# Scan layer: who builds the diagonal blocks of B, GpSimd or ScalarE

## The chip, the core and the metric

The kernel runs on one core of a Trainium2 chip. The metric is the device time of one execution in microseconds (us). Three executions of the kernel before took 9809.74, 9821.51 and 9825.37 us; the median is 9821.51 us.

The engines go by the names of the profile: PE is TensorE (PEld its weight loads), DVE is VectorE, ACT is ScalarE, POOL is GpSimd, SP is SyncE, which here only starts DMAs. Each engine works through its own list of instructions in order and waits on semaphores that the others raise.

## What is computed

`x` is 4 images of 128 channels x 128 x 128 positions. Two layers are added to it, each on a group-normalised input (cut to what matters):

```python
# layer 0, along the 16384 positions of each image
xn = layernorm(gn(x)) * ln_w + ln_b
xin, z = split(xn @ W_in.T)
u = silu(causal_conv4(xin) + conv_b)                 # 256 channels
dt, Bm, Cm = split(u @ W_xproj.T, [8, 24])           # 8, 16 and 16 columns
delta = softplus(dt @ W_dt.T + b_dt)
h = exp(delta * A) * h + (delta * u) * Bm            # 256 channels x 16 states
y = (sum over states of h * Cm + u * D) * silu(z)
x = x + y @ W_out.T
# layer 1: a point-wise network of seven small products with leaky ReLUs; not touched by the change
x = x + sdf(gn(x))
```

## The kernel before

**Two stages per image.** Layer 0 walks the 16384 positions of an image in 32 chunks of 512 (T = 32), layer 1 walks the same 32 chunks after it. The change is in layer 0 alone. Chunks are numbered `t`, with a filling chunk ahead of each image.

**Units.** A chunk's 256 channels x 16 states are 16 units `m` (UNITS = 16). `unit(m)` gives `half`, `gp` (which half of the states) and `q`: units 0 to 3 and 8 to 11 have gp = 0, units 4 to 7 and 12 to 15 have gp = 1. Each unit goes through four engines:

- ACT `decay` (L699): two exponentials of 512 columns, the factor of h, into a ring of four buffers (DR). It may run up to four units ahead of the scan.
- PE `spread` (L446): 32 small products (64 instructions) that multiply delta*u by **diagonal blocks of B** and leave (delta*u)*B in one of two PSUM buffers. `spread(m)` may start when the scan of unit m - 2 is done, as that scan reads the same buffer.
- DVE `scan` (L927): two scans of 512 columns, the recurrence itself.
- POOL `times_c` (L815): one product of 1024 columns, h * C. PE adds these up over the states in `add_states` (L457), four units at a time.

**The order is written out by hand.** Each engine has a function `layer0` with a loop over m = 0 to 15 in which the work of the next two chunks is slipped in at fixed places. PE spreads and ACT decays two units ahead of the loop's m, so that m = 14 and 15 hold units 0 and 1 of the next chunk. What matters here:

- PE: m = 1 `add_states` and `z` half 1 (L401); m = 2 `c_dt_rows` (L406); m = 3 `center_it` (L372); m = 4 `variance` (L378); m = 5 `b_columns` (L414); m = 6 `step_size` (L423); m = 7, 9, 12 `add_states`; m = 8 `project_out` (L470); m = 9 `transpose_du` (L430); m = 11, 13, 15 `conv` (L389), of which m = 15 holds two calls; m = 12 `z` half 0 (L401).
- ACT: every second m `keep_last` (L703), the last state of a pair of units, which waits for their scans; m = 2 `carry_taps` (L633); m = 3 `silu_all` (L639 and L645, with a table load before and after); m = 4 `copy_rows` (L659 to L661); m = 5 `square` (L622); m = 6 `rstd` (L626, L628) and `copy_b` (L667); m = 7 `softplus` (L672 to L676); m = 10 `copy_du` (L681), which waits for `transpose_du`; m = 15 `diagonals` (L689).
- DVE: m = 3 and 12 `gate` (L935, L938); m = 7 `normed` (L911); m = 9 `step_size` (L919); m = 11 `residual` (L943, L945).
- POOL: m = 8 `step_u` (L823), delta*u, which waits for DVE's `step_size` and is what `transpose_du` needs; m = 11, 12 and 15 `diagonals` (L832).

Waits that the change and the prediction speak of: `z` half 1 writes the PSUM bank `qp` that ACT's first silu of z reads, and so waits for it:

```python
def z(t, i, h):
    ...
    if h == 1:
        pe.wait_ge(s_sz, 2 * t + 1)
```

`variance` waits for ACT's `square` (s_sq), ACT's second silu of z waits for `z` half 1 (s_z), `copy_du` waits for `transpose_du` (s_tr), and `transpose_du` waits for `step_u` (s_du).

**The diagonal blocks.** For each chunk b_t (128 x 2 x 4 x 8, written by `copy_b`) holds B's columns. `diag[gp]` is 128 x (4 columns c, 4 rows j, 128): for each c and j, two interleaved 64 x 64 diagonals. Six of the eight quarters (c = 0 to 3 of gp 0, c = 0 and 1 of gp 1) are written by three POOL products of 1024 columns, c = 2 and 3 of gp 1 by 16 ACT copies of 64 columns. A block may only be written anew when the chunk's last spread that reads it is done: for gp 0 that is unit 11 (s_set at 12), for gp 1 unit 15 (s_set at 16). The next chunk's spread of unit 0 waits for the blocks of gp 0, that of unit 4 for those of gp 1.

**SP's queue**, in one chunk: 16 DMAs that replicate delta (L284) in two groups, the load and the store of x (L257, L262), and twice four DMAs that replicate C (L275), of which the second four are needed by POOL's unit 4 of the next chunk.

Of the kernel before, what the change touches and what calls it, by code (L numbers as in the profile page):

```python
# [6 lines left out]
ALU = mybir.AluOpType  # L7
ACT = mybir.ActivationFunctionType

P = 128  # L10
# [4 lines left out]
UNITS = 16  # L15
# [19 lines left out]
def mamba_sdf_kernel(nc, x, w_in_t, conv_w_t, conv_b, ln_w, ln_b, w_cd_t, w_dt_t, a_log,  # L35
# [7 lines left out]
    with ExitStack() as ctx:  # L43
        def sb(name, shape, dt=F32):
            return ctx.enter_context(nc.sbuf_tensor(name, shape, dt))
# [26 lines left out]
        dmask = sb("dmask", [P, 64])  # L72
# [38 lines left out]
        b_t = sb("b_t", [P, 2, 4, 8])  # L111
# [7 lines left out]
        def halves(k):  # L119
# [3 lines left out]
        diag = [over(8 + 4 * i, 4).rearrange("p (c j k) -> p c j k", c=4, j=4) for i in range(2)]  # L123
# [22 lines left out]
        g = [over(40 + i, 1) for i in range(2)]  # L146
# [27 lines left out]
        s_xd, s_rows, s_bt, s_btc = sem("s_c_dt_rows"), sem("s_rows_copied"), sem("s_b_columns"), sem("s_b_copied")  # L174
        s_dt, s_ab, s_ed, s_sp, s_del, s_du = sem("s_dt"), sem("s_abs_dt"), sem("s_exp_dt"), sem("s_log_dt"), sem("s_delta"), sem("s_delta_u")
        s_tr, s_dut, s_dg, s_dga = sem("s_du_transposed"), sem("s_du_t_copied"), sem("s_diagonals"), sem("s_diagonals_by_scalar")
        s_cd, s_cr, s_dr = sem("s_c_stored"), [sem(f"s_c_replicated{i}") for i in range(2)], [sem(f"s_delta_replicated{i}") for i in range(8)]

        s_dA, s_set, s_scan, s_car, s_ch, s_sum = sem("s_decay"), sem("s_dBu"), sem("s_scan"), sem("s_state_carried"), sem("s_Ch"), sem("s_summed")
        s_sk, s_yg, s_o, s_res, s_st1 = sem("s_skip_added"), sem("s_gated"), sem("s_projected"), sem("s_residual"), sem("s_stats1")  # L180

        s_f1, s_f1l = sem("s_f1"), sem("s_f1_leaky")
        s_f2, s_f2l = sem("s_f2"), sem("s_f2_leaky")
# [7 lines left out]
        pe_counts = {s_cen: 1, s_var: 1, s_z: 2, s_cv: 2, s_xd: 1, s_bt: 1, s_dt: 1, s_tr: 1, s_set: UNITS, s_sum: 4, s_o: 1,  # L191
                     s_f1: 1, s_f2: 1, s_gp: 1, s_m2: 2 * NG, s_m3: NG, s_m4: NG // 2}
        act_counts = {s_sq: 1, s_lv: 1, s_rs: 1, s_c3: 1, s_sz: 2, s_u: 2, s_rows: 1, s_btc: 1,
                      s_ab: 1, s_ed: 1, s_sp: 1, s_dut: 1, s_dga: 1, s_dA: 2 * UNITS, s_car: UNITS // 2, s_f1l: 1, s_f2l: 1,
                      s_t2: 2 * NG, s_t3: NG, s_sg: 1}
        pool_counts = {s_du: 1, s_dg: 2, s_ch: UNITS}
        dve_counts = {s_xn: 1, s_del: 1, s_scan: 2 * UNITS, s_sk: 2, s_yg: 2, s_res: 1, s_st1: 1,
# [20 lines left out]
        def real(i):  # L218
            return 0 <= i < T
# [122 lines left out]
        def _(pe):  # L342
# [12 lines left out]
            for h in range(2):  # L355
                m = mm(ps[:, 3, 8 + h:9 + h], w_z[:, h * P:(h + 1) * P], lnb[:, :], start=True, stop=True)
# [76 lines left out]
            def spread(t, i, m):  # L433
                half, gp, q, e = unit(m)
                if m == 0:
                    pe.wait_ge(s_dut, t + 1)
                if m in (0, 4):
                    pe.wait_ge(s_dg, 2 * t + gp + 1)
                if m == 4:
                    pe.wait_ge(s_dga, t + 1)  # L440
                pe.wait_ge(s_scan, 2 * UNITS * t + 2 * (m - 1))
                for c in range(4):
                    for r in range(2):
                        for j in range(4):
                            dst = dbu[m % 2].rearrange("p (r s c g) -> p r c s g", r=2, c=4, g=2)[32 * j:32 * j + 32, r, c, :, :]
                            k = mm(dst,  # L446
                                   du_t[i % 2][64 * r:64 * r + 64, c, 32 * e:32 * e + 32], diag[gp][64 * r:64 * r + 64, c, j, :],
                                   start=True, stop=True)
                k.then_inc(s_set, 1)
# [154 lines left out]
        def _(act):  # L604
            A = nc.scalar.activation
# [57 lines left out]
            def copy_b(t):  # L663
                act.wait_ge(s_bt, t + 1)
                act.wait_ge(s_dg, 2 * t)
                act.wait_ge(s_dga, t)
                A(b_t[:, :, :, :].rearrange("p g c k -> p (g c k)"), pp[:, 1, 0:4 * NS], ACT.Copy).then_inc(s_btc, 1)  # L667

            def softplus(t):
# [8 lines left out]
            def copy_du(t, i):  # L678
                act.wait_ge(s_tr, t + 1)
                act.wait_ge(s_set, UNITS * (t - 1))  # L680
                A(du_t[i % 2].rearrange("p (k c) d -> p k (c d)", k=2), pp, ACT.Copy).then_inc(s_dut, 1)  # L681

            def diagonals(t):
                act.wait_ge(s_btc, t + 1)
                act.wait_ge(s_set, UNITS * t)
                for c in range(2, 4):
                    for j in range(4):
                        for gi in range(2):
                            d = A(diag[1][:, c, j, :].rearrange("p (s g) -> p g s", g=2)[:, gi, :], dmask[:, :], ACT.Copy,  # L689
                                  scale=b_t[:, 1, c, 2 * j + gi:2 * j + gi + 1])  # L690
                d.then_inc(s_dga, 1)

            def decay(t, m):
# [11 lines left out]
            def layer0(b, i):  # L705
                t = b * T + i + 1
                for m in range(UNITS):
                    if m + 2 < UNITS and real(i):
                        decay(t, m + 2)
                    elif m + 2 >= UNITS and real(i + 1):  # L710
                        decay(t + 1, m + 2 - UNITS)
                    if m == 0 and real(i - 1):
                        keep_last(t - 1, UNITS // 2 - 1)
                    if m > 0 and m % 2 == 0 and real(i):
                        keep_last(t, m // 2 - 1)
                    if m == 2 and real(i + 2) and i + 2 > 0:
                        carry_taps(t + 2, i + 2)
                    if m == 3 and real(i + 1):
                        silu_all(t + 1, i + 1)
                    if m == 4 and real(i + 1):  # L720
                        copy_rows(t + 1)
                    if m == 5 and real(i + 2):
                        square(t + 2)
                    if m == 6 and real(i + 2):
                        rstd(t + 2)
                    if m == 6 and real(i + 1):
                        copy_b(t + 1)
                    if m == 7 and real(i + 1):
                        softplus(t + 1)
                    if m == 10 and real(i + 1):  # L730
                        copy_du(t + 1, i + 1)
                    if m == 15 and real(i + 1):
                        diagonals(t + 1)

            def features(t):
                def first_layer():
# [68 lines left out]
        @block.gpsimd  # L805
        def _(pool):
            chunk_zero(pool, pool_counts)

            def times_c(t, m):
                half, gp, q, e = unit(m)  # L810
                if m % 8 in (0, 4):
                    pool.wait_ge(s_cr[gp], 64 * (t + 1))
                pool.wait_ge(s_scan, 2 * UNITS * t + 2 * m + 2)
                pool.wait_ge(s_sum, 4 * t + (m - CR) // 4 + 1)
                nc.gpsimd.tensor_tensor(hc[m % CR], H[:, m % HR, :, :], crep[:, 2 * gp:2 * gp + 2, :], ALU.mult).then_inc(s_ch, 1)  # L815

            def step_u(t, i):
                pool.wait_ge(s_del, t + 1)
                pool.wait_ge(s_u, 2 * t + 2)
                pool.wait_ge(s_tr, t)  # L820
                def fours(v):
                    return v.rearrange("p h (s c) -> p h s c", c=4)
                nc.gpsimd.tensor_tensor(du.rearrange("p h c s -> p h s c"), fours(delta), fours(u[t % 3]), ALU.mult).then_inc(s_du, 1)  # L823

            def diagonals(t, gp, part):
                if part == 0:
                    pool.wait_ge(s_btc, t + 1)
                    pool.wait_ge(s_set, UNITS * (t - 1) + 12 + 4 * gp)
                dst = diag[gp][:, 2 * part:2 * part + 2, :, :].rearrange("p c j (s g) -> p (c j) s g", g=2)
                one = dmask[:, :].rearrange("p (k s g) -> p k s g", k=1, g=1).to_broadcast([P, 8, 64, 2])  # L830
                col = b_t[:, gp, 2 * part:2 * part + 2, :].rearrange("p c (j s g) -> p (c j) s g", s=1, g=2).to_broadcast([P, 8, 64, 2])
                d = nc.gpsimd.tensor_tensor(dst, one, col, ALU.mult)  # L832
                if part == 1 or gp == 1:
                    d.then_inc(s_dg, 1)

            def layer0(b, i):
                t = b * T + i + 1
                for m in range(UNITS):
                    if real(i):
                        times_c(t, m)  # L840
                    if m == 8 and real(i + 1):
                        step_u(t + 1, i + 1)
                    if m == 11 and real(i + 1):
                        diagonals(t + 1, 0, 0)
                    if m == 12 and real(i + 1):
                        diagonals(t + 1, 0, 1)
                    if m == 15 and real(i + 1):
                        diagonals(t + 1, 1, 0)

            for b in range(B):  # L850
                for i in range(-1, T):
                    layer0(b, i)
# [273 lines left out]
```

## Time and profile before

| | us |
|---|---|
| median of three executions | 9821.51 |
| profiled execution, its own time | 9827.07 |
| its span | 9825.2 |
| TensorE clock granted, mean | 0.98 |
| busy: PE | 9314.5 (95%) |
| busy: DVE | 8993.4 (92%) |
| busy: ACT | 8370.6 (85%) |
| busy: POOL | 5791.9 (59%) |

The shares are means over two kinds of stage: POOL works in layer 0 only. The profiled execution lies 5.6 us above the median of the three, its span 1.9 us below its own time. A timeline row gives start, length, engine, line and operation, and in square brackets the idle time before it with what ended it; rows of like instructions are merged, and their number stands behind the x. Instructions of one engine overlap a little, so the pace of a group is read from one row's start to the next row's start.

### The profile page before, as it was taken

What the parts mean: (1) busy time and instruction counts of PE and PEld (TensorE: products, weight loads), DVE (VectorE), ACT (ScalarE), POOL (GpSimd) and SP (SyncE); (2) the same over time, 40 slices, a digit from 0 to 9 for tenths busy, and PEclk for the clock granted to TensorE, in tenths of its full rate; (3) what the DMA queues carried; (4) which work ended last, traced back from release to release, by engine and by line L of the source; (5) the groups of instructions that cost most, each with busy time, mean ns of one, the idle gap of its engine ahead of it and who ended that gap; (6) DMA issues with size and microseconds to landing.
All of it is one profiled execution on the core that took longest, in us unless ns stands there. A gap on an engine that the chain in (4) does not pass through costs nothing. (4 is left out here: it accounts for less than half of the span.)

```text
span 9825.2 us, 453859 instructions
## 1 busy us (share of the span) xinstructions
PE 9314.5 (95%) x201050; PEld 3949.9 (40%) x201050; DVE 8993.4 (92%) x10311; ACT 8370.6 (85%) x14741; POOL 5791.9 (59%) x2564
## 2 busy tenths in 40 slices
PE   7999998999899999899989999989998999998999
PEld 4555553222455555222245555522224555552222
DVE  6999998999699999899979999989997999998998
ACT  5888887999778888799978788879997887887999
POOL 5999993000699999300069999930007999992000
PEclk9999998999999999899999999999999999999999
DMA  3333331000233333100023333310002333321000
GB/s 102 81 82 88 83 84 44 31 31 27 66 81 87 84 81 86 40 31 31 27 69 87 81 81 84 84 43 29 30 27 73 87 81 82 87 80 32 21 22 18
DMA packets 377226, 605.60 MB, mean 62 GB/s; under 512 B 96962, under 2 KB 98148, under 8 KB 374756
## 3 DMA queue, kind: packets, MB, share of 16 engines
q1 hardware_dynamic: 370752, 574.99, 21.0%
q8 instruction: 1587, 26.00, 1.2%
q14 instruction: 371, 3.04, 0.1%
q10 hardware_dynamic: 4516, 1.57, 0.1%
HBM read 236.45 MB, written 71.30 MB: 31 GB/s over the span
## 5 line engine op out<-in xcount | busy, mean ns | idle before, releaser
L927 DVE TENSOR_TENSOR_SCAN arena<-arena,carried,ps 128x512 f32<-128x512 f32 x3968 | 4754.3, 1261 | 294.2 <-PE ps L446 287.9
L815 POOL TENSOR_TENSOR arena<-arena 128x1024 f32<-128x1024 f32 x2048 | 4798.2, 2382 | 148.1 <-PE ps L457 53.2
L975 DVE SCALAR_TENSOR_TENSOR arena<-arena,neg_p 128x512 f32<-128x512 f32 x4096 | 2762.8, 747 | 0.4
L699 ACT ACTIVATE arena<-arena,a_neg 128x512 f32<-128x512 f32 x4096 | 2662.8, 710 | 35.6 <-DVE arena L927 30.8
L446 PE MATMUL ps<-arena 64*32 64x128 f32 x131072 | 2335.8, 275 | 107.9 <-DVE arena L927 57.5
L754 ACT ACTIVATE arena<-ps,b2t 128x512 f32<-128x512 f32 x3840 | 2334.8, 699 | 70.3 <-PE ps L540 44.3
L446 PEld LDWEIGHTS ps<-arena 64*32 64x32 f32 x131072 | 1849.8, 106 | 1234.4 <-DVE arena L927 696.5
L823 POOL TENSOR_TENSOR arena<-arena 128x1024 f32<-128x1024 f32 x128 | 307.6, 2403 | 2969.7 <-DVE arena L919 2968.2
L540 PE MATMUL ps<-arena,w2s 32*32 32x512 f32 x32768 | 1578.5, 603 | 53.6 <-ACT arena L754 35.5
L761 ACT ACTIVATE arena<-ps,bm 128x1024 f32<-128x1024 f32 x1024 | 1165.3, 1138 | 6.1 <-PE ps L551 6.1
L551 PE MATMUL ps<-arena,m 64*32 64x512 f32 x16384 | 1120.7, 599 | 8.6 <-ACT arena L761 4.9
L457 PE MATMUL ps<-arena,sel 128*32 128x512 f32 x8192 | 1013.6, 612 | 37.6 <-POOL arena L815 21.1
L389 PE MATMUL ps<-xnf,w_conv 128*128 128x512 f32 x2048 | 1004.2, 623 | 16.6 <-DVE xnf L911 8.9
L540 PEld LDWEIGHTS ps<-arena,w2s 32*32 32x32 f32 x32768 | 366.6, 103 | 1191.0 <-issue 608.4
L832 POOL TENSOR_TENSOR arena<-dmask,b_t 128x1024 f32<-128x1024 f32 x384 | 735.0, 1915 | 0.0
L551 PEld LDWEIGHTS ps<-arena,m 64*32 64x32 f32 x16384 | 218.8, 104 | 909.3 <-issue 909.3
L681 ACT ACTIVATE arena<-ps 128x1024 f32<-128x1024 f32 x128 | 131.2, 1025 | 524.7 <-PE ps L430 524.7
L689 ACT ACTIVATE arena<-dmask,b_t 128x64 f32<-128x64 f32 x2048 | 504.0, 341 | 63.1 <-PE ps L446 63.1
L561 PE MATMUL ps<-arena,m 128*32 128x512 f32 x4096 | 546.3, 605 | 5.0 <-ACT arena L761 5.0
L389 PEld LDWEIGHTS ps<-xnf,w_conv 128*128 128x128 f32 x2048 | 364.0, 192 | 418.2 <-issue 402.8
L457 PEld LDWEIGHTS ps<-arena,sel 128*32 128x32 f32 x8192 | 228.2, 111 | 465.2 <-issue 432.7
L703 ACT ACTIVATE carried<-arena 128x4 f32<-128x4 f32 x1024 | 202.7, 198 | 248.1 <-DVE arena L927 241.2
(111 smaller groups left out, 6570.0 us busy)
## 6 DMA issues: line engine op xcount, KB each, us to landing
arena<-arena SPq DMA_DIRECT2D x4096, 64.0 KB, 2.0
arena<-c_d SPq DMA_DIRECT2D x1024, 128.0 KB, 2.9
xr<-in_x SPq DMA_DIRECT2D x128, 256.0 KB, 3.2
x_d<-xr SPq DMA_DIRECT2D x128, 256.0 KB, 3.3
xr<-x_d SPq DMA_DIRECT2D x128, 256.0 KB, 3.0
out<-arena SPq DMA_DIRECT2D x128, 256.0 KB, 2.0
xs<-in_x SPq DMA_DIRECT2D x96, 256.0 KB, 3.2
arena<-in_x SPq DMA_DIRECT2D x4, 2048.0 KB, 14.9
```

What stands on the lines that cost most here:

```text
L389: m = mm(pp[:, h, :], w_conv[:, k, h, :], xn[:, k:k + L], start=k == 0, stop=i > 0 and k == TAPS - 1)
L446: k = mm(dst, du_t[i % 2][64 * r:64 * r + 64, c, 32 * e:32 * e + 32], diag[gp][64 * r:64 * r + 64, c, j, :], start=True, stop=True)
L457: m = mm(y_ps[32 * q:32 * q + 32, :], sel[:, :], hc[(4 * k + q) % CR][:, gi, :], start=k % 2 == 0 and gi == 0, stop=k % 2 == 1 and gi == 1)
L540: m = mm(m2_ps[32 * q:32 * q + 32, j, :], w2s[32 * j:32 * j + 32, :], t1[k % 4][32 * j:32 * j + 32, q, :], start=True, stop=True)
L551: m = mm(m3_ps[32 * j:32 * j + 32, r, :], m3[64 * r:64 * r + 64, :], t2[k % 4][64 * r:64 * r + 64, j, :], start=True, stop=True)
L699: A(dA[(UNITS * t + m) % DR][:, gi, :], drep[:, e, :], ACT.Exp, scale=a_neg[:, e, 2 * gp + gi:2 * gp + gi + 1]).then_inc(s_dA, 1)
L754: a = A(t2[k % 4][:, j, :], m2_ps[:, j, :], ACT.Prelu, bias=b2t[:, GQ * k + j:GQ * k + j + 1], alpha=SLOPE)
L761: A(t3[k % 4], m3_ps, ACT.Prelu, bias=bm3[:, :], alpha=SLOPE).then_inc(s_t3, 1)
L815: nc.gpsimd.tensor_tensor(hc[m % CR], H[:, m % HR, :, :], crep[:, 2 * gp:2 * gp + 2, :], ALU.mult).then_inc(s_ch, 1)
L832: d = nc.gpsimd.tensor_tensor(dst, one, col, ALU.mult)
L927: V.tensor_tensor_scan(H[:, m % HR, gi, :], dA[(UNITS * t + m) % DR][:, gi, :], dbu[m % 2].rearrange("p (l g) -> p g l", g=2)[:, gi, :], 0 ...
L975: m = V.scalar_tensor_tensor(out=t1[k % 4][:, q, :], in0=g[par], scalar=neg_p[:, i:i + 1], in1=gs_[par], op0=ALU.max, op1=ALU.add)
```

## The change

Before, POOL made three products per chunk (at m = 11, 12, 15) and ACT sixteen copies (at m = 15). After, POOL makes two products (c = 0 and 1 of gp 0 at m = 11, c = 0 and 1 of gp 1 at m = 15), and ACT makes 32 copies in four calls of eight: gp 0 c = 2 at m = 12, gp 0 c = 3 at m = 13, gp 1 c = 2 at m = 14, gp 1 c = 3 at m = 15, each behind the decay (and keep_last) of its m. Each ACT call waits for b_t and for the old block's last spread. s_dga now counts four per chunk; PE's spread of unit 0 waits for 2 of them and that of unit 4 for all 4.

```diff
 # tensor, spread
                 if m in (0, 4):
                     pe.wait_ge(s_dg, 2 * t + gp + 1)
-                if m == 4:
-                    pe.wait_ge(s_dga, t + 1)
+                    pe.wait_ge(s_dga, 4 * t + 2 * gp + 2)
 # scalar
-            def diagonals(t):
+            def diagonals(t, gp, c):
                 act.wait_ge(s_btc, t + 1)
-                act.wait_ge(s_set, UNITS * t)
-                for c in range(2, 4):
-                    for j in range(4):
-                        for gi in range(2):
-                            d = A(diag[1][:, c, j, :].rearrange("p (s g) -> p g s", g=2)[:, gi, :], dmask[:, :], ACT.Copy,
-                                  scale=b_t[:, 1, c, 2 * j + gi:2 * j + gi + 1])
+                act.wait_ge(s_set, UNITS * (t - 1) + 12 + 4 * gp)
+                for j in range(4):
+                    for gi in range(2):
+                        d = A(diag[gp][:, c, j, :].rearrange("p (s g) -> p g s", g=2)[:, gi, :], dmask[:, :], ACT.Copy,
+                              scale=b_t[:, gp, c, 2 * j + gi:2 * j + gi + 1])
                 d.then_inc(s_dga, 1)
...
+                    if m == 12 and real(i + 1):
+                        diagonals(t + 1, 0, 2)
+                    if m == 13 and real(i + 1):
+                        diagonals(t + 1, 0, 3)
+                    if m == 14 and real(i + 1):
+                        diagonals(t + 1, 1, 2)
                     if m == 15 and real(i + 1):
-                        diagonals(t + 1)
+                        diagonals(t + 1, 1, 3)
 # gpsimd
-            def diagonals(t, gp, part):
-                if part == 0:
-                    pool.wait_ge(s_btc, t + 1)
-                    pool.wait_ge(s_set, UNITS * (t - 1) + 12 + 4 * gp)
-                dst = diag[gp][:, 2 * part:2 * part + 2, :, :].rearrange("p c j (s g) -> p (c j) s g", g=2)
+            def diagonals(t, gp):
+                pool.wait_ge(s_btc, t + 1)
+                pool.wait_ge(s_set, UNITS * (t - 1) + 12 + 4 * gp)
+                dst = diag[gp][:, 0:2, :, :].rearrange("p c j (s g) -> p (c j) s g", g=2)
...
                     if m == 11 and real(i + 1):
-                        diagonals(t + 1, 0, 0)
-                    if m == 12 and real(i + 1):
-                        diagonals(t + 1, 0, 1)
+                        diagonals(t + 1, 0)
                     if m == 15 and real(i + 1):
-                        diagonals(t + 1, 1, 0)
+                        diagonals(t + 1, 1)
```

## Rows read from the trace of the kernel before

**Rows 1.** Busy time in the scan stages of the four images (us; x instructions).

```profile
core 0: us, PE busy (x) PEld busy (x) DVE busy (x) ACT busy (x) POOL busy (x), PEclk, DMA share, GB/s
91.00:1513.50 1422.50, 1371.92 (x35300) 757.48 (x35306) 1339.73 (x1225) 1169.05 (x2281) 1385.32 (x613) 0.99 0.32 84
2528.10:3960.90 1432.80, 1375.56 (x35300) 757.69 (x35308) 1340.06 (x1225) 1169.32 (x2282) 1386.10 (x613) 0.99 0.31 83
4978.70:6409.10 1430.40, 1371.33 (x35300) 756.68 (x35308) 1339.05 (x1225) 1169.25 (x2281) 1385.01 (x612) 0.99 0.31 83
7426.40:8853.70 1427.30, 1371.66 (x35300) 756.75 (x35308) 1339.72 (x1225) 1169.22 (x2282) 1385.71 (x613) 0.99 0.31 83
```

**Rows 2.** Line L681 from 0 to 2000 us: durations (ns), first and last start.

```profile
L681 ACT ACTIVATE arena<-ps x32: 1024/1025/1027, 91.0 to 1513.5; 128x1024 f32<-128x1024 f32 x32
```

**Rows 3.** Timeline of POOL, one chunk.

```profile
1002.90 2.41 POOL L823 TENSOR_TENSOR arena<-arena 128x1024 f32<-128x1024 f32 x1 [0.18 <-DVE arena L919]
...
1016.43 1.93 POOL L832 TENSOR_TENSOR arena<-dmask,b_t 128x1024 f32<-128x1024 f32 x1
1018.29 7.04 POOL L815 TENSOR_TENSOR arena<-arena 128x1024 f32<-128x1024 f32 x3
...
1037.12 11.72 POOL L815 TENSOR_TENSOR arena<-arena 128x1024 f32<-128x1024 f32 x5 [0.61 <-DMA arena<-c_d]
1048.81 2.39 POOL L823 TENSOR_TENSOR arena<-arena 128x1024 f32<-128x1024 f32 x1
```

**Rows 4.** Timeline of ACT, the same chunk, from copy_du to copy_du.

```profile
1007.89 1.02 ACT L681 ACTIVATE arena<-ps 128x1024 f32<-128x1024 f32 x1 [3.77 <-PE ps L430]
...
1015.22 0.21 ACT L703 ACTIVATE carried<-arena 128x4 f32<-128x4 f32 x1 [1.31 <-DVE arena L927]
...
1017.15 3.94 ACT L689 ACTIVATE arena<-dmask,b_t 128x64 f32<-128x64 f32 x16 [0.50 <-PE ps L446]
1020.99 1.32 ACT L699 ACTIVATE arena<-arena,a_neg 128x512 f32<-128x512 f32 x2
...
1027.77 0.69 ACT L639 ACTIVATE arena<-ps,zb 128x512 f32<-128x512 f32 x1
...
1053.34 1.02 ACT L681 ACTIVATE arena<-ps 128x1024 f32<-128x1024 f32 x1 [3.89 <-PE ps L430]
```

**Rows 5.** Timeline of PE, the same chunk.

```profile
1005.80 2.05 PE L430 MATMUL ps<-idn,arena 128*128 128x128 f32 x16
...
1015.88 1.16 PE L446 MATMUL ps<-arena 64*32 64x128 f32 x64
...
1018.88 2.20 PE L446 MATMUL ps<-arena 64*32 64x128 f32 x128
...
1028.60 1.10 PE L401 MATMUL ps<-xnf,w_z 128*128 128x512 f32 x2
...
1036.97 1.12 PE L378 MATMUL ps<-arena,omean 128*128 128x512 f32 x2 [1.07 <-ACT arena L622]
...
1051.25 2.05 PE L430 MATMUL ps<-idn,arena 128*128 128x128 f32 x16
```

**Rows 6.** Waits, window 700 to 1400 us: engine, releaser, total us, times, longest.

```profile
DVE arena L927 <- PE ps L446: 28.0, 56, 1.7
PE ps L378 <- ACT arena L622: 16.0, 15, 1.1
PEld ps L430 <- POOL arena L823: 13.3, 14, 2.3
```

**Rows 7.** Timeline of DVE, the first scans of the next chunk.

```profile
1020.10 4.79 DVE L927 TENSOR_TENSOR_SCAN arena<-arena,carried,ps 128x512 f32<-128x512 f32 x4 [0.22 <-PE ps L446]
```

**Rows 8.** Timeline of PE, a later chunk of the second image.

```profile
3312.24 2.05 PE L430 MATMUL ps<-idn,arena 128*128 128x128 f32 x16
...
3335.31 1.13 PE L401 MATMUL ps<-xnf,w_z 128*128 128x512 f32 x2
...
3343.72 1.12 PE L378 MATMUL ps<-arena,omean 128*128 128x512 f32 x2 [1.07 <-ACT arena L622]
...
3348.99 1.96 PE L446 MATMUL ps<-arena 64*32 64x128 f32 x64
```

**Rows 9.** The page's groups: out<-in xcount | busy, mean ns | idle before, releaser.

```profile
L689 ACT ACTIVATE arena<-dmask,b_t 128x64 f32<-128x64 f32 x2048 | 504.0, 341 | 63.1 <-PE ps L446 63.1
```

More of the change, by code:

```diff
@@ L193, in mamba_sdf_kernel @@
         act_counts = {s_sq: 1, s_lv: 1, s_rs: 1, s_c3: 1, s_sz: 2, s_u: 2, s_rows: 1, s_btc: 1,
-                      s_ab: 1, s_ed: 1, s_sp: 1, s_dut: 1, s_dga: 1, s_dA: 2 * UNITS, s_car: UNITS // 2, s_f1l: 1, s_f2l: 1,
+                      s_ab: 1, s_ed: 1, s_sp: 1, s_dut: 1, s_dga: 4, s_dA: 2 * UNITS, s_car: UNITS // 2, s_f1l: 1, s_f2l: 1,
                       s_t2: 2 * NG, s_t3: NG, s_sg: 1}
@@ L665, in copy_b @@
                 act.wait_ge(s_dg, 2 * t)
-                act.wait_ge(s_dga, t)
+                act.wait_ge(s_dga, 4 * t)
                 A(b_t[:, :, :, :].rearrange("p g c k -> p (g c k)"), pp[:, 1, 0:4 * NS], ACT.Copy).then_inc(s_btc, 1)
@@ L823, in step_u @@
                 nc.gpsimd.tensor_tensor(du.rearrange("p h c s -> p h s c"), fours(delta), fours(u[t % 3]), ALU.mult).then_inc(s_du, 1)
-            def diagonals(t, gp, part):
-                if part == 0:
-                    pool.wait_ge(s_btc, t + 1)
-                    pool.wait_ge(s_set, UNITS * (t - 1) + 12 + 4 * gp)
-                dst = diag[gp][:, 2 * part:2 * part + 2, :, :].rearrange("p c j (s g) -> p (c j) s g", g=2)
+            def diagonals(t, gp):
+                pool.wait_ge(s_btc, t + 1)
+                pool.wait_ge(s_set, UNITS * (t - 1) + 12 + 4 * gp)
+                dst = diag[gp][:, 0:2, :, :].rearrange("p c j (s g) -> p (c j) s g", g=2)
                 one = dmask[:, :].rearrange("p (k s g) -> p k s g", k=1, g=1).to_broadcast([P, 8, 64, 2])
[L831 to L834, printed above, removed]
+                col = b_t[:, gp, 0:2, :].rearrange("p c (j s g) -> p (c j) s g", s=1, g=2).to_broadcast([P, 8, 64, 2])
+                nc.gpsimd.tensor_tensor(dst, one, col, ALU.mult).then_inc(s_dg, 1)
             def layer0(b, i):
```

## The prediction

> **What bounds the kernel now.** I read the busy time by stage first. In the four scan stages POOL is the fullest engine, at 1385 of 1422.5 us in the first, PE and DVE follow with 1372 and 1340, ACT has 1169 [rows 1]. The bounds of these stretches are the first and last `copy_du` (L681) of an image, 32 of them, so 31 chunks [rows 2]: the chunk takes 45.89, 46.22, 46.14 and 46.04 us, mean 46.07. In one chunk (31 to a stretch) PE is busy 44.3 us, DVE 43.2, ACT 37.7. So three engines are nearly full, and ACT has 8.4 us idle. The change takes work from the fullest and gives it to the emptiest.
>
> The shares do not say what sets the pace, so I read one chunk on each engine. POOL runs from one `step_u` (L823) to the next in 1048.81 - 1002.90 = 45.91 us, 0.61 of it a wait for a DMA of C: 45.3 us of work [rows 3]. That would be enough to be the bound. PE, however, has a circle of its own that is as long:
>
> - `transpose_du` (L430) starts at 1005.80, `z` half 1 (L401) at 1028.60: 22.80 us [rows 5];
> - from there to `variance` (L378) at 1036.97: 8.37 us. It ends in a wait for ACT's `square`, 16.0 us in 15 chunks [rows 5, 6];
> - from there to the next L430 at 1051.25: 14.28 us, without a gap on PE [rows 5].
>
> The sum is 45.45 us, the length of the same chunk on ACT, 1007.89 to 1053.34 [rows 4]. POOL's `step_u` holds up the weight load of L430 in 14 of 15 chunks, but for 13.3 us in all, 0.9 each [rows 6], most of which passes while the matrix multiplies of the group before still run. I read it as two circles of nearly equal length, POOL's 45.3 and PE's some 45.3.
>
> In the first leg ACT matters. L401 waits for the bank that ACT's first silu of z (L639) reads. That silu starts at 1027.77 and lasts 0.69, to 1028.46; L401 starts at 1028.60 [rows 4, 5]. So ACT has no slack there, although it idles 8.4 us per chunk: its idle time lies elsewhere, 3.77 us of it just before L681 [rows 4].
>
> **POOL's side.** One product of the diagonal blocks goes. Its pace is 1018.29 - 1016.43 = 1.86 us [rows 3]; POOL's work falls to 43.4 us. What is next late without it is PE's circle. Of that circle only the wait at L430 is POOL's. I take 0.1 us per chunk as the gain (below by 0, above by the 0.9 of the weight load's wait [rows 6]), since L378 to L430 is made of groups that follow each other without a gap. The DMA of C, for which POOL waits 0.61 us here, is not moved earlier, so a faster POOL waits there a little longer, at no cost while POOL has 1.9 us to spare.
>
> **ACT's side.** Sixteen copies more. Sixteen take 1020.99 - 1017.15 = 3.84 us, 0.24 each [rows 4]; the addition is 3.84 us and ACT goes from 37.7 to 41.5 us a chunk, well under 46. By that alone it would be hidden. Where does it lie? All 32 copies stand between L681 (m = 10) and the next chunk's L639 (m = 3), in one queue. That stretch begins when L430 is done (L681 starts 2.09 us after L430's start [rows 4, 5]), and its end releases L401. It is the first leg of PE's circle. The 3.77 us of idle time ahead of L681 cannot cover it, as it ends only when PE has done L430.
>
> Length of that stretch before: 1007.89 to 1028.46, 20.57 us. In it ACT waits 1.31 us for the scan of unit 13 (`keep_last` at m = 14) and 0.50 us for the last spread (L689 at m = 15) [rows 4]. Both waits are absorbed by the new copies ahead of them: the two batches at m = 12 and 13 last 3.84 us, so that `keep_last` comes at 1015.22 - 1.31 + 3.84 = 1017.75, past the end of the scan of unit 13, for which it waited until 1015.22. The batch of m = 14 waits for the spread of unit 15, which runs from 1015.88 for 1.16 us, to 1017.04 [rows 5]: done, so it waits for nothing either. The stretch is then work alone:
>
> 20.57 - 1.31 - 0.50 + 3.84 = 22.60 us. I take 22.4, an estimate that lets some 0.1 us of gap at each of the two waits go with them.
>
> First leg after: 2.09 + 22.4 + 0.14 (L639's end to L401's start) = 24.6 us, against 22.80. The second leg, 8.37, begins with L401 and consists of ACT's work behind it (second silu, table load, rows, `square`): unchanged. The third: 14.28 - 0.1. The new circle is 24.6 + 8.4 + 14.2 = 47.2 us against 45.45: +1.75. In a later chunk the first leg was 3335.31 - 3312.24 = 23.07 [rows 8], which gives +1.5.
>
> Does the delay turn back later on? The decay of the next chunk's unit 0 stands just ahead of that `keep_last`, so it is done by 1017.75; its scan starts at 1020.10 [rows 7]. The second batch stands ahead of that decay, and the spread of unit 0, which now waits for it, belongs to the row of 1018.88 [rows 5]; the spread of unit 4 comes behind L401, and the last batch is long over by then. So the waits that are added cost nothing on PE. SP has nothing behind them: its next wait on a decay is for that of unit 15, done by then. The ACT queue behind the batches (decays, `keep_last`, `carry_taps`, silu) moves as a whole, and the first that anyone waits for is the silu of z.
>
> **From one chunk to the mean.** The mean chunk is 46.07, 0.6 over the clean one. Some of it is PE itself standing still: in the later chunk one spread took 1.96 us instead of 1.16 [rows 5, 8]. After the change such a hold-up in the first leg (half of the chunk) is covered, as PE has up to 1.75 us to spare there; in the other two legs it still counts. So I keep about 0.25 of the 0.6: 47.2 + 0.25 = 47.45, less 46.07 = +1.38 us per chunk. Between all of it absorbed (47.0, +0.9) and none (47.8, +1.8) this is the middle, somewhat to the low side: I take +1.35. Times 31 x 4 = 124 chunks: +167 us. The filling chunk of each image and layer 1 do not change.
>
> 9827.07 (the profiled execution) + 167 = 9994; as that execution lies 5.6 us above the median of the three, the forecast against the median is 9821.5 + 167 = 9988, say 9988 us, +1.7%.
>
> **The rivals.**
>
> *A, faster: POOL sets the pace.* For it: POOL is fullest [rows 1], its work of 45.3 us is within 0.15 us of the clean chunk [rows 3], and L430 waits for it in nearly every chunk [rows 6]. Then the chunk could fall by 1.86 us until the next engine stops it, PE with 44.3 us busy [rows 1] plus the same 0.6 of hold-ups, 44.9: -1.17 x 124 = -145 us, 9676. Against it: DVE waits 28.0 us for PE in these 15 chunks [rows 6] and for POOL not at all, and even with a faster POOL the path over ACT is 47.2 long. It decides only if ACT's first silu could come 1.8 us later without L401 moving, which the 0.14 us between them speaks against.
> The Trainium skill, page "Perfetto Trace Analysis", section "Identifying the Most-Contended Engine", says to take the engine with the highest occupancy as the one to relieve first. By that rule this case is A. I give the circle more weight.
>
> *B, no change: the extra copies are hidden.* If PE came so late to L401 that ACT's delay did not show, by a longer spread-and-conv part at m = 15, the time stays within 20 us: 9820. For it: the later chunk has 0.4 us of such slack. Against: 1.5 us would be needed.
>
> *C, slower still.* The copies in four batches do not overlap at their ends: a single copy lasts 0.341 us against a pace of 0.24 [rows 4, 9], so at most 0.1 more per batch, 0.4 per chunk; and waits of ACT inside the stretch come back when PE is late. With +2.3 us per chunk: +285 us, 10107.
>
> **How the numbers follow.** Forecast 0.80, A 0.08, B 0.07, C 0.05. About 0.2% (20 us) is what can be told from no change. Faster 0.08, same 0.07, slower 0.85. Own range of the forecast: +0.9 to +1.8 us per chunk and a margin for what I did not see in PE's third leg, 9895 to 10065. A and B lie outside, with C they hold the 2 in 10.
>
> **What would show it.** Right: chunk of 47 to 47.6 us; L430 to L401 24.4 to 24.7 us in nearly every chunk; L401 <- ACT L639 becomes the largest wait of PE, 1.5 us a chunk; ACT without idle time from L681 to L639; POOL with 3 to 4 us of idle time per chunk, waiting for scans; DVE's waits for PE up by about as much as the chunk. Wrong: a chunk below 46, L401 not waiting for ACT, or copies with another pace than 0.24 us.

## The result and the profile after

The changed kernel takes 9934.51 us (median of four, 9932.66 to 9948.14) against 9815.74 us (median of four): ratio 1.012, 95% interval 1.0107 to 1.0132. It is slower, as forecast, by 119 us instead of the 167 forecast, and lies inside the range.

The page, first the shares. PE and POOL are busy for less time than before, DVE for 15 us more; ACT has 16 more instructions a chunk (16789 - 14741 = 2048, by 128 chunks).

```profile
span 9932.4 us, 456291 instructions
PE 9288.5 (94%) x201050; PEld 3939.6 (40%) x201050; DVE 9008.9 (91%) x10311; ACT 8816.1 (89%) x16789; POOL 5568.2 (56%) x2436
```

The page's groups (busy and mean, then the idle time before and its releaser): twice as many copies at the same price, one third of the POOL products gone, and a wait of L401 for ACT of 169.4 us in the run, which was 8.8 before.

```profile
L819 POOL TENSOR_TENSOR arena<-arena 128x1024 f32<-128x1024 f32 x2048 | 4805.1, 2380 | 458.0 <-PE ps L456 157.4
L687 ACT ACTIVATE arena<-dmask,b_t 128x64 f32<-128x64 f32 x4096 | 1031.2, 342 | 0.0
L835 POOL TENSOR_TENSOR arena<-dmask,b_t 128x1024 f32<-128x1024 f32 x256 | 491.1, 1919 | 0.0
L401 PE MATMUL ps<-xnf,w_z 128*128 128x512 f32 x512 | 289.0, 646 | 169.9 <-ACT arena L638 169.4
```

The copy_du line (L681 before, L680 after), in four answers for the four images, gives the mean chunk; it answers to [rows 2].

```profile
L680 ACT ACTIVATE arena<-ps x32: 1024/1025/1030, 91.0 to 1546.9; 128x1024 f32<-128x1024 f32 x32
L680 ACT ACTIVATE arena<-ps x32: 1024/1025/1027, 2560.5 to 4014.2; 128x1024 f32<-128x1024 f32 x32
L680 ACT ACTIVATE arena<-ps x32: 1024/1026/1031, 5031.6 to 6486.2; 128x1024 f32<-128x1024 f32 x32
L680 ACT ACTIVATE arena<-ps x32: 1024/1025/1030, 7499.6 to 8954.3; 128x1024 f32<-128x1024 f32 x32
```

By 31 these are 46.96, 46.89, 46.92 and 46.93 us, against 46.07 in the mean before: +0.86 us, times 124 chunks 107 us, and the span grew by 9932.4 - 9825.2 = 107.2 us (12 less than the medians, as the profiled execution before, 9827.07 us, lies 11 above the median of its four). The whole loss lies in the scan chunks.

One chunk on PE, answering to [rows 5]:

```profile
1010.91 1.12 PE L378 MATMUL ps<-arena,omean 128*128 128x512 f32 x2 [1.07 <-ACT arena L621]
...
1025.07 2.05 PE L430 MATMUL ps<-idn,arena 128*128 128x128 f32 x16
...
1049.48 1.10 PE L401 MATMUL ps<-xnf,w_z 128*128 128x512 f32 x2 [1.70 <-ACT arena L638]
...
1057.85 0.70 PE L378 MATMUL ps<-arena,omean 128*128 128x512 f32 x1 [1.07 <-ACT arena L621]
```

The three legs are 14.16, 24.41 and 8.37 us, in sum 46.94. Before they were 14.28, 22.80 and 8.37. Only the leg with the copies has grown, and its growth shows as PE's wait of 1.70 us. On ACT (answering to [rows 4]) the same stretch has no idle time in brackets any more, and the four batches stand in it (the first three are shown):

```profile
1027.15 1.02 ACT L680 ACTIVATE arena<-ps 128x1024 f32<-128x1024 f32 x1 [3.78 <-PE ps L430]
...
1030.62 2.01 ACT L687 ACTIVATE arena<-dmask,b_t 128x64 f32<-128x64 f32 x8
1032.54 1.32 ACT L697 ACTIVATE arena<-arena,a_neg 128x512 f32<-128x512 f32 x2
1033.76 2.01 ACT L687 ACTIVATE arena<-dmask,b_t 128x64 f32<-128x64 f32 x8
1035.67 1.32 ACT L697 ACTIVATE arena<-arena,a_neg 128x512 f32<-128x512 f32 x2
1036.90 0.19 ACT L701 ACTIVATE carried<-arena 128x4 f32<-128x4 f32 x1
1036.99 2.01 ACT L687 ACTIVATE arena<-dmask,b_t 128x64 f32<-128x64 f32 x8
...
1048.64 0.69 ACT L638 ACTIVATE arena<-ps,zb 128x512 f32<-128x512 f32 x1
```

The window 700 to 1400 us, answering to [rows 6]: POOL now waits, most of all for the DMAs of C. L401's wait is new.

```profile
DVE arena L926 <- PE ps L445: 44.3, 89, 1.4
PE ps L401 <- ACT arena L638: 24.2, 15, 1.7
POOL arena L819 <- DMA arena<-c_d: 21.2, 15, 3.0
POOL arena L819 <- PE ps L456: 17.7, 14, 1.3
PE ps L378 <- ACT arena L621: 16.1, 15, 1.1
PEld ps L430 <- POOL arena L827: 11.7, 14, 0.8
```

### The profile page after: what moved, and what is told of

Same layout as the page of the kernel before. It is cut to its first block and busy times, and to the rows that moved or that the text cites. A ratio compares the mean times of both kernels' runs of the same rounds, so it can differ in the third digit from the quotient of the medians.

```text
span 9932.4 us, 456291 instructions
## 1 busy us (share of the span) xinstructions
PE 9288.5 (94%) x201050; PEld 3939.6 (40%) x201050; DVE 9008.9 (91%) x10311; ACT 8816.1 (89%) x16789; POOL 5568.2 (56%) x2436
## 5 line engine op out<-in xcount | busy, mean ns | idle before, releaser
L687 ACT ACTIVATE arena<-dmask,b_t 128x64 f32<-128x64 f32 x4096 | 1031.2, 342 | 0.0
L680 ACT ACTIVATE arena<-ps 128x1024 f32<-128x1024 f32 x128 | 131.3, 1026 | 504.2 <-PE ps L430 504.2
L835 POOL TENSOR_TENSOR arena<-dmask,b_t 128x1024 f32<-128x1024 f32 x256 | 491.1, 1919 | 0.0
L401 PE MATMUL ps<-xnf,w_z 128*128 128x512 f32 x512 | 289.0, 646 | 169.9 <-ACT arena L638 169.4
```

Of the source, the lines that this page charges most:

```text
L687: d = A(diag[gp][:, c, j, :].rearrange("p (s g) -> p g s", g=2)[:, gi, :], dmask[:, :], ACT.Copy, scale=b_t[:, gp, c, 2 * j + gi:2 * j + g ...
```

## The experiments

Chunk figures in the text are from the timeline's starts of copy_du: the mean over an image or over all 124 chunks, and the clean chunk, a length to which many of them agree within 0.05 us (111 of the changed kernel's 124; 28 of the kernel before, whose others are mostly longer). The first chunk of an image is shorter in every run: 40.8 to 43.8 us before, 43.3 to 44.2 after. "Later chunks" are the other 120. Whether the clock fell in a chunk is read from the granted clock over that chunk alone.

### One part of the change at a time

**e1_pool_only.** POOL's product for c = 2 and 3 of gp 0 only in the first chunk; the later ones use its blocks, so that part of B is left out.

```diff
-                    if m == 12 and real(i + 1):
+                    if m == 12 and real(i + 1) and t + 1 == 1:
                         diagonals(t + 1, 0, 1)
...
-                if part == 1 or gp == 1:
+                if part == 1 or gp == 1 or t > 1:
                     d.then_inc(s_dg, 1)
```

> The kernel before with POOL's product for c = 2 and 3 of gp 0 made in the first chunk only (later chunks read the old blocks: that part of B is left out). ACT is unchanged. Circle theory (PE and ACT set the chunk, POOL only touches it at transpose_du): the clean chunk stays at 45.2 to 45.33 us, mean chunk 45.9 to 46.1, the time 0 to 15 us less, ratio 0.998 to 1.000. POOL theory (POOL's 45.3 us of work is the bound): chunk down by 1.2 us or more, 145 us less, ratio 0.985.

Measured: 9797.5 us, ratio 0.9981 (0.9973 to 0.9990). The clean chunk stays at 45.32 us, exactly that of before, though POOL now has 43.4 us of work. The means of the four images are 45.49, 45.96, 45.76 and 45.94, 0.28 lower than before on the average. Taking 1.86 us from the fullest engine gave 0.2%, not 1.5%: rival A falls. Not all of the 0.28 is POOL's: in the profiled executions the clock falls in 13 of the 120 later chunks here and in 19 before, and the chunks without such a fall take 45.76 against 45.87 us.

**e2_act16.** The kernel before with the same number of copies more, POOL untouched.

```diff
...
+            def spare(k):
+                for j in range(4):
+                    for gi in range(2):
+                        A(spare_t[:, k, 2 * j + gi, :], dmask[:, :], ACT.Copy, scale=dsk[:, gi:gi + 1])
...
+                    if m == 12 and real(i + 1):
+                        spare(0)
+                    if m == 13 and real(i + 1):
+                        spare(1)
```

> The kernel before, POOL's three products kept, with 16 more ACT copies of 64 columns into a spare tile, eight at m = 12 and eight at m = 13. Circle theory: all of the change's loss is here, L430 to L401 is 24.4 us, chunk 46.95, ratio 1.012 as for the changed kernel. If POOL's relief had been paying back a part of ACT's cost in the changed kernel, this one is slower than it: up to 48 us a chunk, ratio 1.02 and more.

("48 us a chunk" there means a chunk of 48 us.) Measured: 9950.63 us, ratio 1.0139 (1.0123 to 1.0155); clean chunk 46.94, the same as the changed kernel's. So ACT's side makes the whole of the clean chunk's growth. POOL's relief is worth at most some 16 us in the changed kernel (9950.6 - 9934.5; the intervals of the two ratios overlap a little) and some 20 us alone. In the two traces even that isn't in the undisturbed chunks, 46.94 here and 46.93 in the changed kernel, but in the number of later chunks in which the clock falls, 18 against 8; that POOL's product has to do with this number is not shown.

### Where the copies stand

**e3_act8** and **e4_act24** are e2 with `spare` at m = 12 only, and at m = 12, 13 and 14.

> The kernel before with 8 more ACT copies into a spare tile at m = 12. Circle theory: the two waits of ACT in the stretch (1.31 + 0.50 us) take 1.81 of the 1.92 us, clean chunk up by 0.1 to 0.2 us, mean chunk by no more than that, ratio 1.000 to 1.003. A theory in which each copy costs its share of the change's loss: half of it, ratio 1.006.

Measured: 9815.82 us, ratio 1.0000 (0.9991 to 1.0009). Eight copies cost nothing: the waits inside the stretch take them.

> The kernel before with 24 more ACT copies into a spare tile, eight each at m = 12, 13 and 14. Circle theory: the waits in the stretch are used up, so the last eight cost their full 1.92 us: chunk 46.94 + 1.92 = 48.86, time some 238 us above e2's 9951, 10185 to 10195, ratio 1.038. Series of spare copies in the stretch: 8, 16, 24 give 0, 1.6, 3.5 us a chunk. A cost that follows their number from the first on (1.6 us for 16) gives 2.4 us a chunk, ratio 1.021.

Measured: 10359.83 us, ratio 1.0548 (1.0530 to 1.0566). The time is a miss: 10185 to 10195 was expected. The clean chunk is 48.85, as expected to 0.01 us, but only some 30 of the 124 have it: the mean chunk of the four images is 50.25 us. The copies are at their expected price, and something else is added behind PE's wait. Timeline of PE in one such chunk:

```profile
3339.68 2.05 PE L402 MATMUL ps<-xnf,w_z 128*128 128x512 f32 x2 [3.38 <-ACT arena L640]
3341.65 1.96 PE L447 MATMUL ps<-arena 64*32 64x128 f32 x64
3343.54 2.87 PE L407 MATMUL ps<-arena,w_cd 128*104 128x512 f32 x4
3346.34 1.16 PE L447 MATMUL ps<-arena 64*32 64x128 f32 x64
```

The same three groups take 1.10, 1.16 and 1.96 us elsewhere. The busy times by window, with the granted clock in the third column from the end, show why:

```profile
3331.00:3337.00 6.00, 5.29 (x148) 2.56 (x146) 4.57 (x5) 6.00 (x17) 6.00 (x4) 1.00 0.32 80
3337.00:3340.00 3.00, 0.33 (x1) 0.36 (x2) 2.97 (x4) 2.97 (x5) 3.00 (x3) 0.76 0.40 98
3340.00:3343.00 3.00, 3.00 (x58) 1.50 (x65) 0.02 (x1) 1.91 (x4) 3.00 (x2) 0.50 0.59 165
3343.00:3346.00 3.00, 3.00 (x28) 1.06 (x12) 2.28 (x2) 2.18 (x4) 0.93 (x1) 0.60 0.02 5
3346.00:3349.00 3.00, 3.00 (x105) 1.71 (x110) 1.62 (x3) 2.51 (x5) 2.36 (x1) 1.00 0.00 0
```

The clock falls inside the 3.38 us without a multiply, is granted at 0.50, 1.2 GHz of 2.4, and is back at 1.00 by 3346; the shares of the three windows add up to 6.8 us at the lower level. The count over all later chunks says how much of the miss this is: in 29 of the 120 the clock doesn't fall, and their mean is 48.85 us; in the other 91 it does, and theirs is 50.90.

**e7_spare_m10.** The sixteen spare copies of e2, at m = 10 ahead of copy_du.

```diff
                     if m == 10 and real(i + 1):
+                        spare(0)
+                        spare(1)
                         copy_du(t + 1, i + 1)
```

> The kernel before with the same 16 more ACT copies into a spare tile as e2, all at m = 10 ahead of copy_du; POOL keeps its three products. Circle theory: the 3.8 us wait for transpose_du hides 3.84 us, ratio 1.000 (up to 1.002), against e2's 1.014 for the same copies at m = 12 and 13. A theory of cost by number gives 1.014 again.

Measured: 9818.18 us, ratio 1.0001 (0.9992 to 1.0009), against 1.0139 for the same sixteen at m = 12 and 13. So the cost of these copies is their place in ACT's queue; their number costs nothing that can be told from noise.

**e5_early.** The changed kernel with the gp 0 batches there.

```diff
                     if m == 10 and real(i + 1):
+                        diagonals(t + 1, 0, 2)
+                        diagonals(t + 1, 0, 3)
                         copy_du(t + 1, i + 1)
-                    if m == 12 and real(i + 1):
-                        diagonals(t + 1, 0, 2)
-                    if m == 13 and real(i + 1):
-                        diagonals(t + 1, 0, 3)
```

> The changed kernel with both batches of gp 0 moved to m = 10, ahead of copy_du, where ACT waits 3.8 us for transpose_du; the batches of gp 1 stay at m = 14 and 15. Same work on every engine. Circle theory: the stretch from L681 to L639 is that of the kernel before, chunk 45.2 to 45.4 clean and 46.0 in the mean, ratio 0.998 to 1.001. If the number of copies on ACT matters and not their place: 1.012. If POOL's relief is worth its 1.86 us once ACT is out of the way: 0.985.

Measured: 9879.32 us, ratio 1.0063 (1.0050 to 1.0075), a miss. The timeline of ACT shows what was overlooked:

```profile
3323.34 3.95 ACT L687 ACTIVATE arena<-dmask,b_t 128x64 f32<-128x64 f32 x16
3327.19 1.00 ACT L680 ACTIVATE arena<-ps 128x1024 f32<-128x1024 f32 x1
...
3334.42 0.21 ACT L701 ACTIVATE carried<-arena 128x4 f32<-128x4 f32 x1 [1.23 <-DVE arena L924]
3336.36 2.03 ACT L687 ACTIVATE arena<-dmask,b_t 128x64 f32<-128x64 f32 x8 [1.73 <-PE ps L445]
3338.29 1.32 ACT L697 ACTIVATE arena<-arena,a_neg 128x512 f32<-128x512 f32 x2
```

The first two rows are as meant: sixteen copies end where copy_du can start. But with them gone from the stretch, ACT is early at m = 14, and the gp 1 batch there waits 1.73 us for the last spread with a decay of 1.23 us behind it, where the kernel before did that decay first and then waited 0.50 [rows 4]. That wait is 1.23 us longer than the one it replaces; the clean chunk grew by 1.05, from 45.33 to 46.38, as two other waits of the stretch, both for scans, became some 0.2 us shorter together.

**e6_early15.** e5 with both gp 1 batches at m = 15, behind that decay.

```diff
-                    if m == 14 and real(i + 1):
-                        diagonals(t + 1, 1, 2)
                     if m == 15 and real(i + 1):
+                        diagonals(t + 1, 1, 2)
                         diagonals(t + 1, 1, 3)
```

> The changed kernel with both batches of gp 0 at m = 10 ahead of copy_du and both batches of gp 1 at m = 15, behind the decay, where the kernel before had its sixteen. Circle theory with the queue's place counted (e5's batch at m = 14 waited 1.73 us for the last spread with the decay of m = 15 stuck behind it): clean chunk 45.33 to 45.45, L401's wait for ACT gone, time as for the kernel with POOL's product left out, ratio 0.997 to 1.000. If ACT's 32 copies cost something wherever they stand, it stays at e5's 1.006.

Measured: 9790.88 us, ratio 0.9972 (0.9959 to 0.9985); clean chunk 45.32. This version beats both kernels, the one before by 0.3% and the changed one by 1.4%, with the same instructions on every engine as the latter. Its timeline of ACT has the wait of 0.50 us again:

```profile
3288.87 3.94 ACT L687 ACTIVATE arena<-dmask,b_t 128x64 f32<-128x64 f32 x16
3292.71 1.00 ACT L680 ACTIVATE arena<-ps 128x1024 f32<-128x1024 f32 x1
...
3301.93 3.94 ACT L687 ACTIVATE arena<-dmask,b_t 128x64 f32<-128x64 f32 x16 [0.50 <-PE ps L445]
```

### The two circles

**e8_pool_plus.** A fourth POOL product per chunk, into a spare tile.

```diff
...
                 if part == 1 or gp == 1:
                     d.then_inc(s_dg, 1)
+                if part == 1:
+                    nc.gpsimd.tensor_tensor(spare_t[:, :, :, :], one, col, ALU.mult)
```

> The kernel before with a fourth POOL product of 1024 columns (into a spare tile, behind the product at m = 12); ACT and PE unchanged. Two circles of equal length (POOL's work 45.3 us, PE's and DVE's 45.3 us): the added 1.86 us of POOL count in full although the same 1.86 us taken away brought nothing in the clean chunk: clean chunk 47.2 us, mean 47.2 to 47.3, some 145 us more, ratio 1.014 to 1.016. If POOL has slack of its own (its weight-load wait at L430 being all it does), the chunk grows by less than 1 us, ratio below 1.008.

Measured: 9950.43 us, ratio 1.0136 (1.0119 to 1.0153). The mean chunk is 46.90 us; 74 of the 124 take 47.0, against 47.2 expected. So 1.86 us more on POOL cost 130 us and 1.67 in the clean chunk, 1.86 us less brought 20 and nothing in the clean chunk. Before the change POOL's circle was within some 0.2 us of PE's: it binds as soon as it grows by more than that, and gives nothing when only it shrinks. That PE's circle alone would give nothing either follows from the same lengths, but no run shortened it.

**e9_z_later.** The changed kernel with `z` half 1 at m = 2 of PE, behind the spread of unit 4.

```diff
-                    if m == 1 and real(i + 1):
+                    if m == 2 and real(i + 1):
                         z(t + 1, i + 1, 1)
```

> The changed kernel with z half 1 (L401) moved on PE from m = 1 to m = 2, behind the spread of unit 4, so that PE does that spread while it waits for ACT's silu. Circle theory: the cost is the length of ACT's queue from copy_du to square, not PE standing at L401; the wait shrinks by about 1.1 us, the chunk stays 46.9 to 47.0 us, ratio 1.011 to 1.013. If PE's idle time at L401 is the cost (the blocked spread of unit 4 holding up DVE), some 1.1 us a chunk comes back, ratio 1.000 to 1.002.

Measured: 10200.31 us, ratio 1.0375 (1.0353 to 1.0398), outside both. Three legs of one chunk:

```profile
3305.54 2.05 PE L430 MATMUL ps<-idn,arena 128*128 128x128 f32 x16
...
3329.95 1.10 PE L401 MATMUL ps<-xnf,w_z 128*128 128x512 f32 x2 [0.36 <-ACT arena L638]
...
3338.32 2.07 PE L378 MATMUL ps<-arena,omean 128*128 128x512 f32 x2 [2.12 <-ACT arena L621]
3340.33 1.68 PE L445 MATMUL ps<-arena 64*32 64x128 f32 x64
...
3353.95 1.27 PE L430 MATMUL ps<-idn,arena 128*128 128x128 f32 x9
```

L430 to L401 is 24.41 and L401 to L378 8.37 us, both those of the changed kernel, and 27 of the 124 chunks take 46.94 us again: on ACT's queue the move changed nothing, as the circle theory says. The wait at L401 shrank from 1.70 to 0.36 us. But PE's idle time went over to L378, which waited 1.07 us in every chunk and now waits 2.12 here, and behind that wait PE runs slower (2.07 us for 1.12): the third leg is 15.6 here. Windows of the same chunk, the granted clock as above:

```profile
3330.00:3336.00 6.00, 6.00 (x136) 2.88 (x136) 5.95 (x7) 5.82 (x10) 4.38 (x2) 1.00 0.44 134
3336.00:3342.00 6.00, 3.88 (x82) 1.98 (x67) 2.91 (x3) 4.86 (x9) 5.30 (x3) 0.72 0.03 8
3342.00:3348.00 6.00, 6.00 (x160) 3.40 (x156) 5.86 (x6) 4.19 (x6) 4.05 (x2) 1.00 0.01 3
```

The rival that PE's pause at L401 was the cost is refuted by the first leg and by the chunks of 46.94 us; the total can't tell, as the clock is in it. In 38 of the 120 later chunks the clock doesn't fall, and their mean is 47.02 us, near the changed kernel's 46.93; in the other 82 it is 50.28. So the miss is the clock's.

## Why the prediction was right, step by step

- *The circle over ACT sets the chunk.* Right. Legs forecast 24.6, 8.4 and 14.2, measured 24.41, 8.37 and 14.16 us; L401 waits for ACT in all 15 chunks of the window, 1.6 us each (24.2 / 15). e2 has it with ACT's side alone, e7 loses it by the place alone.
- *The two waits in the stretch absorb 1.81 us.* Right, and a little more: e3's 1.92 us cost nothing, the changed kernel's 3.84 raised the clean chunk by 1.61 (45.33 to 46.94), so that 2.2 were absorbed, and e4's last 1.92 raised it by 1.91.
- *The stretch as work: 22.4 us.* Measured from 1027.15 to 1048.64 + 0.69 = 1049.33: 22.18. The 0.2 us deducted for short gaps should have been 0.4. Each of the two waits takes 0.1 us more with it than its bracket says, because instructions that needn't wait overlap the one before by that much, and a third, too short for a bracket, went as well: in the kernel before the next `keep_last` starts 1024.92 - 1022.32 = 2.60 us behind its decays, after 2.45. This is the first mis-sized term, 0.2 of the 0.5 us a chunk by which the forecast was high.
- *POOL's relief, 0.1 us a chunk.* Near in size, not right in place. By the medians it is 0.17 in e1 (21.5 us / 124) and 0.13 between e2 and the changed kernel (16 us / 124); in the later chunks in which the clock doesn't fall it is 0.11 and 0.01. It was forecast ahead of L430, but from L378 to L430 those chunks take 14.20 us before and 14.19 in e1; what e1 gains lies in the first leg, 23.29 to 23.21.
- *Hold-ups that remain: 0.25 us.* Wrong in size, and the larger term. The later chunks take 46.22 us in the mean before and 47.04 after, 0.89 and 0.10 above the clean ones. (That the mean of all 124 chunks after, 46.93, is the clean chunk's length is chance: the four short first chunks cancel what the hold-ups add.) There are two kinds of them, and I had taken them for one.

  The first is PE standing still inside a spread with nothing that the profile shows to wait for. This row of the kernel before is one:

```profile
238.22 0.44 PE L446 MATMUL ps<-arena 64*32 64x128 f32 x13 [1.01 <-issue]
```

  In the whole run such idle time at the spreads is 43.8 us before and 28.6 after. The chunks in which the clock doesn't fall show what hold-ups other than the clock's cost: 45.87 us before, 0.54 above the clean one, and 46.93 after, nothing. Their legs before are 23.29, 8.40 and 14.20 us against 22.80, 8.37 and 14.16 in clean chunks: 0.49 of the 0.54 lie in the first leg, where I had put half, and there PE's new wait covers them. What causes this kind is not shown.

  The second is the clock. The spread of 1.96 us in [rows 8], which I took for PE standing still, has no gap in it; it and the group behind it (2.67 us, elsewhere 1.92) are slow, and from 3348 to 3351 us the granted clock was 0.67:

```profile
3350.88 2.67 PE L457 MATMUL ps<-arena,sel 128*32 128x512 f32 x16
3348.00:3351.00 3.00, 3.00 (x73) 1.86 (x76) 3.00 (x4) 2.26 (x3) 3.00 (x3) 0.67 0.03 5
```

  The clock falls in 19 of the 120 later chunks before (mean 48.11 us), which makes 0.35 us a chunk, and in 8 after (48.54), which makes 0.11. This part of the drop is not to be credited to the change or to the forecast: e2, with the same circle of 46.94 us, has 18 such chunks.
- *The DMA of C costs nothing.* Right: POOL waits 21.2 us for it in the window, 3.2 before, and in that window only the weight load of L430 waits for POOL, 11.7 us in all against 13.3.
- *The signs.* POOL's idle time is 4.0 us a chunk in the scan stages, as forecast, but it waits for DMAs of C and for PE before scans. DVE's waits for PE rose by 1.1 us a chunk ((44.3 - 28.0) / 15).
- *Rivals.* A is refuted by e1 and e6: with ACT out of the way POOL's relief gives 0.2 to 0.3%, not 1.5. The Trainium skill's rule of the highest occupancy (page "Perfetto Trace Analysis", section "Identifying the Most-Contended Engine") picks POOL; for this kernel, whose engines form circles of nearly one length, e1 and e6 contradict it. B would have needed 1.5 us of slack, and e2 and the changed kernel show the path over ACT with none of that size. C's dearer copies at the ends of the batches did not come: each batch took 1.91 to 1.92 us, its copies 0.24 each.

## What to carry to other kernels

An engine that idles has room only where it idles: find the wait in its queue (here 3.8 us ahead of copy_du) and put the new work right ahead of it, because the same sixteen copies cost 1.4% a few places further on (e2) and nothing there (e7). When two circles are of nearly one length, relieving one brings little (0.2% here); price an offload by the path of the receiving engine before the share of the giving one. When work leaves a queue, look at the waits it had been covering: e5 lost 1 us a chunk to one of them. And before a mean is compared with a clean chunk, look at single chunks: here short first chunks, PE's standing still and the clock are three different things in one mean.

## What the hardware showed unexpectedly

TensorE's clock falls inside this dense loop, and much more often when the loop holds longer pauses. In the kernel before PE's regular wait is 1.07 us at L378, and the granted clock falls in 19 of 120 later chunks; in the chunk of [rows 8] it does so while PE is at work. In the changed kernel PE waits 1.70 us at L401 besides, the 5 us behind the wait shown above are granted 1.00, and the clock falls in 8 chunks (in 18 of e2, with the same waits). With a wait of 2.12 us at L378 (e9) it falls in 82 chunks: in the one shown the 6 us around and behind the wait are granted 0.72, and the next product takes 2.07 us instead of 1.12. With 3.38 us (e4) it falls in 91, and is at 0.50 for a whole 3 us of the one shown. Why it falls in one chunk and not in the next of the same shape is not shown.

The price comes on top of the pause: later chunks with a fall are 2.0 us longer than those without in e4 (50.90 against 48.85) and 3.3 in e9 (50.28 against 47.02), and the mean granted clock of the run is 0.958 and 0.956, against 0.983 in the changed kernel. Between the changed kernel and e9 the idle time of a chunk at L401 and L378 is about the same (1.70 + 1.07 us and 0.36 + 2.12), and the second costs 266 us more in the run.
